# Attention scores with a block-diagonal k: one 128-row product for four heads, and a redrawn schedule

## What is computed

```python
# block 1: linear attention with gelu features and rotary positions
q = gelu(x @ Wq.T + bq) + 0.21;  k = gelu(x @ Wk.T + bk) + 0.21;  v = x @ Wv.T + bv
z = 1 / (einsum(q, mean_n(k)) + 1e-6);  out = (rope(q) @ (rope(k).T @ v)) * z   # per head
x = LN(x + LN(out + x) * gamma + beta)
# block 2: cross attention on the context
scores = Q @ K.T / sqrt(8)            # per head, 128 x 77
x = LN(x + softmax(scores) @ V @ Wo + bo)
# block 3: 16 experts, gelu, hidden 256, all computed, the top 4 weighted
c = top4(softmax(x @ router_w + router_b)), normalised
x = LN(x + sum_e c_e * (gelu(x @ w1_e + b1_e) @ w2_e + b2_e))
```

## Time and profile before

| | us |
|---|---|
| median of 3 runs | 633.91 (633.74 to 634.24) |
| profiled execution | 632.64 |
| its span | 630.6 |
| TensorE busy | 591.0 (94%) |
| VectorE busy | 418.8 (66%) |
| ScalarE busy | 406.4 (64%) |
| GpSimd busy | 242.8 (38%) |

### The profile page before, as it was taken

One profiled execution on the slowest core, in us unless ns is written; L12 is line 12 of the kernel. 1 busy time (PEld: TensorE's weight loads), 2 busy tenths in 40 slices (PEclk: granted clock), 3 DMA queues, 4 the chain that ended last, 5 costly groups with the idle time before them and its releaser, 6 DMA issues. The chain is left out here.

```text
span 630.6 us, 16584 instructions
## 1 busy us (share of the span) xinstructions
PE 591.0 (94%) x6513; PEld 431.7 (68%) x6513; DVE 418.8 (66%) x1472; ACT 406.4 (64%) x519; POOL 242.8 (38%) x166
## 2 busy tenths in 40 slices
PE   5897988999999999999999999999999999899995
PEld 2543654777668867777677867886778766676664
DVE  2356576666786788677877678678867775365445
ACT  2307727796559856786569665985579657965651
POOL 5235333343253435253444325343425342134242
PEclk9888998999999999999999999999999999999999
DMA  6632020010200120011100120012000110000000
GB/s 145 183 86 76 32 60 28 20 29 1 70 20 3 46 61 28 4 45 29 51 12 2 55 60 19 4 45 65 25 3 19 29 43 5 19 1 2 1 18 18
DMA packets 31541, 23.05 MB, mean 37 GB/s; under 512 B 2744, under 2 KB 30152, under 8 KB 31464
## 3 DMA queue, kind: packets, MB, share of 16 engines
q1 hardware_dynamic: 24120, 16.75, 9.2%
q10 hardware_dynamic: 6992, 4.81, 2.7%
q0 software_dynamic: 352, 0.43, 0.4%
HBM read 13.90 MB, written 5.46 MB: 31 GB/s over the span
## 5 line engine op out<-in xcount | busy, mean ns | idle before, releaser
L713 ACT ACTIVATE g<-ps,b 128x512 f32<-128x512 f32 x256 | 168.2, 686 | 86.2 <-PE ps L1000 85.0
L533 POOL TENSOR_TENSOR gl<-g,gh 128x1024 f16<-128x1024 f32 x64 | 138.3, 2161 | 212.4 <-ACT gh L702 212.4
L1358 DVE SCALAR_TENSOR_TENSOR acc<-ps,cw,acc 128x128 f32<-128x128 f32 x448 | 125.4, 342 | 103.0 <-PE ps L1023 57.3
L1023 PEld LDWEIGHTS ps<-w,g 128*128 128x128 f32 x1024 | 121.6, 192 | 9.8 <-issue 4.6
L1023 PE MATMUL ps<-w,g 128*128 128x128 f32 x1024 | 127.0, 277 | 0.1
L998 PE MATMUL ps<-x2h,w1h 128*128 128x512 f16 x256 | 98.2, 384 | 8.8 <-ACT g L713 8.1
L999 PE MATMUL ps<-x2l,w1h 128*128 128x512 f16 x256 | 97.6, 381 | 0.0
L1000 PE MATMUL ps<-x2h,w1l 128*128 128x512 f16 x256 | 97.5, 381 | 0.0
L1019 PE MATMUL ps<-w2h,gh 128*128 128x128 f16 x512 | 89.2, 219 | 1.7 <-DVE acc L1358 1.5
L1021 PE MATMUL ps<-w2h,gl 128*128 128x128 f16 x512 | 89.0, 219 | 0.0
L1020 PE MATMUL ps<-w2l,gh 128*128 128x128 f16 x512 | 89.0, 219 | 0.0
(11 more groups left out here) (188 smaller groups left out, 864.6 us busy)
## 6 DMA issues: line engine op xcount, KB each, us to landing
q_rep<-q_parts SPq DMA_DIRECT2D x24, 128.0 KB
x<-in_x SPq DMA_DIRECT2D x8, 256.0 KB, 3.3
w_stage<-in_L_ffn_w ACTq DMA_DIRECT2D x1, 2048.0 KB, 13.2
q_swap<-q SPq DMA_DIRECT2D x16, 128.0 KB, 2.4
q_parts<-qx SPq DMA_DIRECT2D x16, 128.0 KB, 1.7
k_rep<-k_parts SPq DMA_DIRECT2D x24, 77.0 KB
out<-fin SPq DMA_DIRECT2D x7, 256.0 KB, 2.5
cx<-in_ctx SPq DMA_DIRECT2D x8, 154.0 KB
```

The source lines that it names most:

```text
L533: pool.tensor_tensor(gl[:, j % SPLIT_RING, :, :], g32[:, e % RING, :, :], gh[:, j % SPLIT_RING, :, :], ALU.subtract).then_inc(s["lo"], 1)
L713: act.activation(g32[:, e % RING, h, :], bH[:, h, :], ACT.Gelu, bias=b1[:, e, h:h + 1], scale=1.0 / WS).then_inc(s["gelu"], 1)
L1023: m = pe.matmul(o, g32[:, e % RING, h, tok], w2[:, j, h, :], start=(h == 0), stop=(h == HALF - 1))
L1358: m = dve.scalar_tensor_tensor(out=(acc_all if e == E - 1 else acc)[:, b, :], in0=second_bank(f, e)[:, b * P:(b + 1) * P], scalar=cw[:, b, ...
```

## The change

`k_rep` gets a dimension of strips: for each block and sequence it holds 4 x 77 columns, and strip r's rows are filled only in the columns of r; elsewhere it holds zero. One product of all 128 rows of q_rep with 308 columns then gives the scores of four heads, one bank for each block i: 4 products for a sequence instead of 16. VectorE's maximum reads the banks in the new order. SP fills the diagonal blocks by 12 DMAs (8 rows, 16 runs of 77 numbers each) instead of 3, k is stored by two DMAs instead of one, and `zero` reads zeros out of k_rep's blocks off the diagonal, so that `zero_rows` goes. The constant rows are set by VectorE at the start (5 memsets), not by four activations on ScalarE. `scores_t` is as before. All tables of places are redrawn: steps move on every engine, and the idle products and the loads and splits of the weights too. Cut to its core:

```diff
 WS = 256.0
 MAX_SCALE = 64.0
 SETS = 4
+STRIPS = 4
...
-SPREAD = 16 * (2 * 3 + 2)
+SPREAD = 16 * (3 * STRIPS + 3 + 2)
...
-    max_rows = np.zeros((P, 1), np.float32)
-    for row in MAX_ROWS:
-        max_rows[row::32] = -MAX_SCALE
     cols = dict(ident=ident, cos=cos2, sin_neg=-sin, sin=sin, cos_t=cos2.T, sin_t=sin_t,
-                same_head=same_head, head_of=head_of,
-                max_rows=max_rows)
+                same_head=same_head, head_of=head_of)
...
-PE_AT = dict(x_t=1, q=4, kv01=6, kv23=13, k_mean=29, kv=32, den=33, out=36, cx_t=43, v1=46, x1_t=58, k=54,
-             q_x=63, scores=(8, 8, 12, 12, 16, 17, 20, 23), max_t=25, scores_t=(31, 33, 38, 40), values=(37, 39,
-             41, 41), wo=54, x2_t=61, logits=0, c_t=58, b2=61, first=3, next=0, second=0, u_t=(42, 47), ao_t=49)
-ACT_AT = dict(x_t=0, q=2, kv23=28, cx_t=45, x1_t=61, k=55, q_x=63, max_t=27, scores_t=(32, 37, 39, 40), x2_t=61,
-              weights=0, c_t=59, gelu=1, high=3, u=(40, 45), ao_t=52)
-DVE_AT = dict(q=11, kv01=5, kv23=25, k_rot=25, k_mean=27, kv=30, den=31, out=36, norm1=37, norm2=39, x1=51,
-              v1=49, k=56, q_x=63, scores=(8, 8, 9, 15, 15, 19, 20, 21), max=24, pairs=(42, 47), wo=56, x2=60,
-              x2_t=62, logits=0, weights=1, cw=11, b2=61, combine=0, finish=40, q_sin=19, sums=33, xl=0,
-              cw_hl=50)
-POOL_AT = dict(x_beta=19, k_rot=25, q_rot=20, res=28, norm1=34, norm2=46, x1=11, x2=61, finish=37, low=2)
-
-PE_FIRST = dict(x_t=4, q=4, kv01=9, cx_t=6, kv23=26, v1=13, k=32, k_mean=36, kv=43, den=46, out=49, x1_t=51,
-                q_x=55)
-PE_EARLY = dict(scores=(0, 0, 0, 0, 0, 0, 0, 0), max_t=11, scores_t=(23, 25, 31, 39), values=(30, 38, 45, 48),
-                u_t=(48, 49), ao_t=59, wo=59, x2_t=63)
-PE_ONE = dict(x_t=0, q=0, kv01=0, kv23=7, k_mean=21, kv=24, den=26, out=33, cx_t=49, v1=50, k=53, x1_t=61,
-              q_x=63)
...
-ACT_ZERO = dict(x_t=3, q=11, kv23=20, cx_t=48, x1_t=62, k=55, q_x=63, max_t=22, scores_t=(29, 30, 35, 37),
-                x2_t=63, weights=0, c_t=53, gelu=3, high=3, u=(36, 45), ao_t=52)
...
+PE_AT = dict(x_t=3, q=6, kv01=9, kv23=15, k_mean=29, kv=30, den=32, out=36, cx_t=43, v1=45, x1_t=59, k=49,
+             q_x=63, scores=(7, 8, 12, 14, 15, 20, 20, 23), max_t=27, scores_t=(29, 35, 38, 40), values=(37, 39,
+             41, 42), wo=54, x2_t=61, logits=3, c_t=56, b2=63, first=3, next=0, second=0, u_t=(42, 47), ao_t=52)
+ACT_AT = dict(x_t=0, q=9, kv23=17, cx_t=41, x1_t=58, k=52, q_x=62, max_t=26, scores_t=(31, 38, 39, 40), x2_t=61,
+              weights=8, c_t=57, gelu=1, high=3, u=(40, 41), ao_t=52)
+DVE_AT = dict(q=17, kv01=10, kv23=15, k_rot=26, k_mean=29, kv=29, den=32, out=33, norm1=39, norm2=40, x1=52,
+              v1=45, k=50, q_x=63, scores=(5, 9, 11, 13, 13, 18, 18, 23), max=24, pairs=(45, 45), wo=53, x2=60,
+              x2_t=62, logits=4, weights=6, cw=11, b2=61, combine=0, finish=43, q_sin=28, sums=29, xl=1,
+              cw_hl=43)
+POOL_AT = dict(x_beta=0, k_rot=25, q_rot=26, res=26, norm1=30, norm2=39, x1=46, x2=54, finish=32, low=2)
+
+PE_FIRST = dict(x_t=2, q=11, kv01=11, cx_t=6, kv23=12, v1=24, k=30, k_mean=27, kv=30, den=34, out=42, x1_t=45,
+                q_x=56)
+PE_EARLY = dict(scores=(0, 0, 0, 0, 0, 0, 0, 0), max_t=3, scores_t=(12, 28, 32, 40), values=(31, 39, 41, 45),
+                u_t=(48, 51), ao_t=53, wo=57, x2_t=62)
+PE_ONE = dict(x_t=0, q=0, kv01=0, kv23=1, k_mean=6, kv=26, den=32, out=36, cx_t=44, v1=45, k=52, x1_t=53,
+              q_x=62)
...
+ACT_ZERO = dict(x_t=0, q=12, kv23=29, cx_t=45, x1_t=61, k=48, q_x=63, max_t=25, scores_t=(31, 35, 38, 44),
+                x2_t=63, weights=3, c_t=60, gelu=3, high=3, u=(42, 46), ao_t=52)
...
-PE_FILL0 = dict(q=2, kv01=12, kv23=0, k_mean=0, kv=0, den=0, out=2, v1=0, k=10, x1_t=50, q_x=1)
-PE_FILL1 = dict(q=8, kv01=5, kv23=0, scores=0, max_t=1, scores_t=4, kv=11, den=0, out=0, k_mean=7, values=0,
-                wo=3, q_x=1, x2_t=0, v1=0, x1_t=15, u_t=43)
-
-HIGH_W = (28, 67, 73, 77, 77, 85)
-LOW_W = (33, 67, 90, 91, 116, 126)
-SCALE_W = (49, 105)
-LOAD_W = (25, 26, 45, 74)
-W1_W = (7,)
-ROWS_W = (16, 11)
+PE_FILL0 = dict(q=5, kv01=10, kv23=3, k_mean=6, kv=5, den=0, out=0, v1=2, k=3, x1_t=49, q_x=3)
+PE_FILL1 = dict(q=14, kv01=8, kv23=0, scores=0, max_t=0, scores_t=1, kv=11, den=2, out=1, k_mean=2, values=61,
+                wo=1, q_x=3, x2_t=14, v1=3, x1_t=13, u_t=36)
+
+HIGH_W = (48, 67, 70, 74, 75, 108)
+LOW_W = (37, 41, 60, 71, 90, 125)
+SCALE_W = (117, 122)
+LOAD_W = (30, 43, 44, 46)
+W1_W = (6,)
+ROWS_W = (58,)
...
-        k_rep = sb("k_rep", [P, BLK, B * CTX], F16)
+        k_rep = sb("k_rep", [P, BLK, B, STRIPS, CTX], F16)
         q_rep = sb("q_rep", [P, BLK, T], F16)
-        zero_rows = sb("zero_rows", [4, BLK, T], F16)
...
-        k_parts = nc.dram_tensor("k_parts", (P, 2, B * CTX), F16, kind="Internal").ap()
+        k_parts = nc.dram_tensor("k_parts", (P // BLK, 2, BLK, B, CTX), F16, kind="Internal").ap()
...
-                    sp.dma_start(q_rep[row_at::32, :, :], zero_rows[:, :, :]).then_inc(s["ld_rep"], 16)
+                    sp.dma_start(q_rep[row_at::32, :, :].rearrange("p i (a n) -> p (i a) n", n=P),
+                                 k_rep[0:STRIPS, :, :, 1:3, :].rearrange("p i b r n -> p (i b) (r n)")[:, :, 0:P]).then_inc(s["ld_rep"], 16)
...
                 since(sp, "ld_rep", SPREAD * a)
                 since(sp, "kxh", a + 1)
                 since(sp, "kxl", a + 1)
-                sp.dma_start(k_parts, kx[:, :, :]).then_inc(s["st_k"], 16)
+                for t in range(2):
+                    sp.dma_start(k_parts.rearrange("r t i b n -> i r t (b n)")[:, :, t, :], kx[:, t, :]).then_inc(s["st_k"], 16)
 
             def spread_k(a):
 
                 since(sp, "t_p", B * a)
-                since(sp, "st_k", 16 * (a + 1))
-                by_block = k_parts.rearrange("(i r) t n -> r i t n", i=BLK)
+                since(sp, "st_k", 2 * 16 * (a + 1))
                 for n in (0, 2, 1):
-                    sp.dma_start(k_rep[n::SETS, :, :], by_block[:, :, int(n == 1), :]).then_inc(s["ld_rep"], 16)
+                    for r in range(STRIPS):
+                        sp.dma_start(k_rep[32 * r + n:32 * (r + 1):SETS, :, :, r, :].rearrange("p i b n -> p (i b) n"),
+                                     k_parts[8 * r:8 * (r + 1), int(n == 1), :, :, :].rearrange("r i b n -> r (i b) n")).then_inc(s["ld_rep"], 16)
...
                 if p == ROWS_W[0]:
-
-                    act.wait_ge(s["ld_c"], 16)
-                    for i in range(BLK):
-                        act.activation(k_rep[:, i, :], cst[:, 0:B * CTX], ACT.Identity, bias=c_("max_rows"), scale=0.0).then_inc(s["i_rows"], 1)
-                if p == ROWS_W[1]:
                     act.wait_ge(s["i_rw"], 16)
...
@@ -916,10 +910,9 @@
                     since(pe, "ld_rep", SPREAD * (g + 1))
                 else:
                     since(pe, "mx", 2 * (B * g + b - 1) + half + 1)
-                for r in (2 * half, 2 * half + 1):
-                    for i in range(BLK):
-                        m = pe.matmul(ps[:, r, i * CTX:(i + 1) * CTX], q_rep[32 * r:32 * r + 32, i, b * P:(b + 1) * P],
-                                      k_rep[32 * r:32 * r + 32, i, b * CTX:(b + 1) * CTX], start=True, stop=True)
+                for i in (2 * half, 2 * half + 1):
+                    m = pe.matmul(ps[:, i, 0:STRIPS * CTX], q_rep[:, i, b * P:(b + 1) * P],
+                                  k_rep[:, i, b, :, :].rearrange("p r n -> p (r n)"), start=True, stop=True)
                 m.then_inc(s["s_p"], 1)
...
-                        m = pe.matmul(ps[0:CTX, r, i * P:(i + 1) * P], k_rep[32 * r:32 * r + 32, i, b * CTX:(b + 1) * CTX],
+                        m = pe.matmul(ps[0:CTX, r, i * P:(i + 1) * P], k_rep[32 * r:32 * r + 32, i, b, r, :],
...
                         if p == at["scores"][2 * b + half]:
                             since(dve, "s_p", 2 * n + half + 1)
                             since(dve, "mxl", g)
-                            dve.tensor_reduce(mx[:, b, HEADS // 2 * half:HEADS // 2 * (half + 1)].rearrange("p (r i) -> p r i", r=2),
-                                              ps[:, 2 * half:2 * half + 2, 0:BLK * CTX].rearrange("p r (i k) -> p r i k", i=BLK),
+                            two = slice(2 * half, 2 * half + 2)
+                            dve.tensor_reduce(mx[:, b, :].rearrange("p (r i) -> p i r", r=STRIPS)[:, two, :],
+                                              ps[:, two, 0:STRIPS * CTX].rearrange("p i (r k) -> p i r k", r=STRIPS),
                                               AX.X, ALU.max).then_inc(s["mx"], 1)
...
             dve.memset(q_rep[:, :, :], 0.0).then_inc(s["i_rows"], 1)
-            dve.memset(zero_rows[:, :, :], 0.0).then_inc(s["i_rows"], 1)
+            dve.memset(k_rep[:, :, :, :, :], 0.0).then_inc(s["i_rows"], 1)
+            dve.wait_ge(s["i_rows"], 2)
+            for r in range(STRIPS):
```

(33 more changed lines are left out.)

22 lines of the change are left out of this document (5 added, 17 removed).

## The result

The changed kernel takes 655.27 us (median of 4 runs, 651.35 to 657.56) for 633.85 (4 runs on the same chip, 633.74 to 634.24): a ratio of 1.033, 95% interval 1.0296 to 1.0364. It is 3.3% slower; I had forecast 625.5.

What follows compares the result with a forecast made beforehand. TensorE, busy 94% of the span, was taken as the bound. From the profiled 632.64 us, scores -0.6, pass gap -5.8, first group -2.0 and start 0 gave 624.2, or 625.5 for the median; range 620.5 to 631.5.

Steps and rivals of the forecast that it cites:

- DMAs, taken as hidden: Each group's SP queue: 12 DMAs for 3 spreading k, 2 for 1 staging it, claimed to cost no time.
- first rival: On SP, k's spread delays q's copies and the scores wait: +10 us, 643 us; chance 0.08.
- price d: SP's issue time per k spread DMA: 0.65 us assumed; waiting begins near 0.75, the gained 0.9 us shrinks from 0.84.
- f = 0: First group's feed-forward pass: its dearer wait between expert 0 and expert 1 shrinks, 2.0 us gained.
- The start, 0 between -4 and +4: Kernel start, with redrawn fills, loads and k_rep setting: gains and losses of 1 to 4 us each, net 0.
- second rival: The start loses 3 to 4 us by later ao_t and low-clock fills, cancelling group gains: 629 to 630; chance 0.15.
- The gap at the pass's start: TensorE's 0.83 us idle between expert 0 and expert 1 closes with logits and th moved: -5.8 us over seven groups.
- kv at place 30: In each group kv loses an expert's 1.3 us cover: a wait of some 0.2 us, given back later.
- my seven groups: Groups f = 1 to 7, each claimed to gain 0.83 us at the start of the feed-forward pass: -5.8 us.
- Scores: Score products on TensorE: 2.08 us a group for 2.14 in strips, -0.08 with small gaps, -0.6 us over 8 groups.

Runs made afterwards that it cites:

- k in 4 spreads: The changed kernel with k staged in DRAM as whole rows, 3 stores and 4 spread DMAs of 512 runs instead of 2 and 12 of 128; 629.70 us (0.994).

## Why the prediction was wrong

*DMAs, taken as hidden: this step failed, and carries the groups' loss.* The mechanism was written down as the first rival, with its place and its sign, and given 0.08. Its working was short by 2.4 us: it had SP free 1.6 us ahead of expert 0, and it was free 0.8 behind it. Counted against expert 0, kx was complete within 0.2 us of where I had it; two stores and their landing took 4.0 us where I put 2.5; twelve spreads at 0.70 instead of 0.65 are 0.6; the rest is small gaps. So the price d, which I took for the unknown, was nearly right (0.70, with the break-even by my sum at 0.84), and the store's landing, which I carried over from a contiguous store (2.15 us in all), was the term that was off. Behind SP it went on: q's store took 2.72 us to its spread. A margin of 0.5 us behind a chain of sixteen DMAs should not have carried 0.65 of the chance. Two sizes in that rival are also wrong, though no sum uses them: one of q_rep's three DMAs carries 128 KB, not 43, and k's spreads 231 KB a group, not 77.

*f = 0* was to gain 2.0 us. Its own gain is real but smaller, about 1.5 (68.1 for 69.6 us with k in 4 spreads); in the changed kernel a wait of 4.7 us for q's copies of the second group stands in front, and the clock behind it is at its lower level: 4.6 lost.

*The start, 0 between -4 and +4, was +7.2.* New places alone +5.0, new products alone +3.1. I had called VectorE's setting of k_rep hidden; it was not (wql at 12.97 for 10.41; it took 4.17 us where I put 2.2), but a run showed that it costs nothing behind the wait for cx. What cost is that x(1), the x of the second group, is loaded behind the long first spread (issued at 46.45 for 39.40 before; TensorE waits 2.7 us for it, and the granted clock from 40 to 60 us is 0.95 and 0.88); with 4 spreads that wait is gone, the clock there is 1.00, and the start is 3.7 us shorter. Of the places, x1_t with its 13 fills and VectorE's kx and x1 ahead of ao_t are 3.2 us of the order; moving them away cost 2.1 in f = 0 and didn't shorten the time beyond the noise. The clock falls between the maxima and the transposed scores, the point I named in the second rival; that the missing fills are the reason is not shown. How the rest is shared out stays open: the clock falls at other points from run to run, and single profiles of the start differ by 3 us (101.3 and 104.7 for two kernels that do the same there).

*The gap at the pass's start* closed as worked out, 0.83 us, ScalarE's wait for `lgm` from 17.7 to 0.0. *kv at place 30* cost 0.3, near the 0.2 said: kv waits 0.30 us for k_mean in five groups, where before it doesn't wait, and this isn't given back at the next wait for the exps (0.28 for 0.27 before). *f = 7 gained nothing*, against my seven groups: 54.6 us for 54.5 from expert 0 on, though expert 1 starts 0.46 earlier: TensorE then waits 0.9 us for VectorE's acc_all once in that pass (the row below is the changed kernel's), a wait that the kernel before doesn't have.

```profile
PE ps L1016 <- DVE acc_all L1352: 0.9, 1, 0.9
```


*Scores: right in mechanism, mis-sized.* 0.131 us apart and no gap at either end, as said. But I priced the strips at 2.14 us a group; a visit in strips also makes a product behind it late, by 0.10 us twice a group, and the new places have a seventh visit. New products against old in the new places is 0.7 us a group, not 0.08; the places alone give 0.4, not 0.8. The sum, 1.05, came out near the forecast (67.4 us for 67.5), by two errors that cancel; that is luck. The Trainium skill's rule of TensorEngine Tiling (Array Packing), Theoretical Speedup, that strips of 32 rows gain up to 4 times, would have made the groups 1.6 us longer; the trace shows them 0.7 shorter with the same places (67.4 for 68.1).

With q in time, then, the groups are as forecast, and the kernel with 4 spreads takes 0.994 of the time before. Of the 4.2 us that its 629.70 is above 625.5, 3.5 stand in the start (expert 0 of f = 0 at 97.6 for 94.1).
